# Opening loop of a graph layer: statistics one block at a time, loads spread between the stores, deeper table rows, list work in quarters

## The reference

```python
xn = _layernorm(x, axis=-1)                     # (6250, 256)
h  = (xn @ W).reshape(n, 8, 32)                 # L0_gnn
a1 = jnp.sum(h * attn_l, axis=-1); a2 = jnp.sum(h * attn_r, axis=-1)
e  = leaky_relu(a1[src] + a2[dst]);  out = segment_sum(h[src] * softmax_by_dst(e), dst)
q, k, v = split(xn_normalised @ Wqkv);  k = softmax(k, axis=nodes)      # L0_mix
```

## Time and profile before

| | |
|---|---|
| time, median of 3 runs | 6431.17 us (6430.95 to 6431.87) |
| time of the profiled execution | 6432.53 us, its span 6430.7 us |
| opening loop, first instruction of turn 0 to that of turn 48 (VectorE) | 19.93 to 185.11 us |
| mean granted clock of TensorE | 0.885 of full speed |
| busy in the whole span: TensorE, VectorE, GpSimd, ScalarE | 4977.0, 4128.9, 3649.1, 1548.3 us |

### The profile page before, as it was taken

The page is one execution under the profiler, slowest core; times in us unless marked ns, Lnnn a source line. Parts: engine busy times, 40 slices in busy tenths (PEclk is TensorE's granted clock), DMA queues, the critical chain, the costliest instruction groups (busy, mean ns, idle before and its releaser), DMA issues. The chain is left out here.

```text
span 6430.7 us, 105194 instructions
## 1 busy us (share of the span) xinstructions
PE 4977.0 (77%) x26438; PEld 3591.3 (56%) x26691; DVE 4128.9 (64%) x9565; ACT 1548.3 (24%) x3076; POOL 3649.1 (57%) x3844
## 2 busy tenths in 40 slices
PE   5867777777777776799799997777777777766694
PEld 4535555555555555798544444655555555555583
DVE  5438999998989898435650003877777777666444
ACT  1213333333333333454433331000000000000341
POOL 3447777777777773603200004777777777776524
PEclk8978999989888887799999998888888888888597
DMA  4424444444444443423344443333333333333345
GB/s 144 125 72 109 113 113 113 113 113 113 113 113 113 113 112 117 143 77 103 106 149 169 174 171 126 109 109 109 109 109 109 109 109 109 106 105 96 131 147 151
DMA packets 367220, 762.40 MB, mean 119 GB/s; under 512 B 92003, under 2 KB 232321, under 8 KB 354241
## 3 DMA queue, kind: packets, MB, share of 16 engines
q0 software_dynamic: 175104, 491.59, 27.1%
q1 hardware_dynamic: 184912, 262.86, 12.1%
q10 hardware_dynamic: 7056, 6.43, 0.3%
HBM read 562.75 MB, written 199.66 MB: 119 GB/s over the span
## 5 line engine op out<-in xcount | busy, mean ns | idle before, releaser
L868 POOL DMA_INDIRECT rg_ring<-y_dram,src_at x1612 | 1528.3, 948 | 1265.2 <-POOLq L906 774.3
L868 POOL DMA_INDIRECT ga_ring<-h_dram,src_at x1612 | 1532.6, 951 | 507.9 <-issue 460.8
L1716 PE MATMUL rg_psS<-rg_ring,rg_hot_w 128*128 x4000 | 1148.1, 451 | 397.7 <-SPq L844 304.2
L1716 PEld LDWEIGHTS rg_psS<-rg_ring,rg_hot_w 128*128 128x128 f32 x4000 | 902.0, 230 | 640.2 <-issue 478.1
L1042 PE MATMUL ga_psS<-ga_msg,ga_hot 128*128 128x280 f32 x4000 | 1194.1, 455 | 46.1 <-DVE ga_msg L1182 38.1
L1042 PEld LDWEIGHTS ga_psS<-ga_msg,ga_hot 128*128 128x128 f32 x4000 | 850.0, 221 | 313.9 <-DVE ga_msg L1182 88.6
L1833 DVE TENSOR_SCALAR rg_hot_t<-rg_psB,pair_node,place 128x1024 bf16<-128x1024 f32 x253 | 338.4, 1338 | 586.0 <-PE rg_psB L915 586.0
L1521 PE MATMUL rr_psY<-rr_wr,rr_xt 128*128 128x512 f32 x1568 | 675.1, 593 | 4.6 <-DMA rr_xt<-x_dram 4.6
L1182 DVE SCALAR_TENSOR_TENSOR ga_msg<-ga_psW,ga_ring 128x2112 f32<-128x2112 f32 x251 | 587.3, 2340 | 0.0
L1521 PEld LDWEIGHTS rr_psY<-rr_wr,rr_xt 128*128 128x128 f32 x1568 | 298.4, 190 | 379.0 <-issue 373.9
L2261 PE MATMUL f_psH<-f_xt,f_now 128*128 128x128 f32 x2688 | 351.3, 281 | 48.9 <-DVE f_now L2554 37.9
(11 more groups left out here) (403 smaller groups left out, 6694.3 us busy)
## 6 DMA issues: line engine op xcount, KB each, us to landing
y_dram<-rr_y SPq DMA_DIRECT2D x98, 1024.0 KB
f_x<-xg_dram SPq DMA_DIRECT2D x224, 128.0 KB
yg_dram<-f_work SPq DMA_DIRECT2D x224, 128.0 KB
ga_ring<-h_dram,src_at POOLq DMA_INDIRECT x1612
rg_ring<-y_dram,src_at POOLq DMA_INDIRECT x1612
rr_xt<-x_dram SPq DMA_DIRECT2D x98, 128.0 KB, 3.8
f_w<-L_ffn_W SPq DMA_DIRECT2D x16, 512.0 KB, 6.0
h_dram<-op_row SPq DMA_DIRECT2D x49, 136.0 KB, 1.8
```

The costliest lines, as they stand in the source:

```text
L868: p.indirect_dma_start(ring[:, (g % R) * G + j, :], None, table, bass.IndirectOffsetOnAxis(ap=rows[:, g * G + j:g * G + j + 1], axis=0)).t ...
L1716: o = pe.matmul(psS[:, u % 2, 0:C], hot_w[:, u % 2, j, :], rows[:, j, :], start=j == 0, stop=j == G - 1)
```

## The change

It changes only the opening's first block, apart from three counts in the next one.

- **Statistics.** The blocks are in seven groups of seven. `measure(b)` does one `bn_stats`; two follow each of turns 0 to 5, then one each turn, until turn 35. `spreads` (the small operations) follows turns 3, 7, 14, 21, 28 and 35, and `scales_of` (wait for the root, reciprocals) one turn later. ScalarE's `root_of` stands after turns 3, 7, 14, 21, 28 and 35.
- **Loads.** Two groups of x are loaded ahead of the loop, the others after the stores of turns 0, 2, 7, 12 and 17. The node list comes in four quarters after turns 9, 14, 18 and 20, the source list and late weights after turn 22. SyncE issues a turn's turned block ahead of its table row.
- **Table rows.** `row` has four buffers instead of two, with a semaphore each.
- **List work.** The node list's mask and conversion are done a quarter at a time, mask and conversion in alternate turns, over turns 24 to 31; the pair lists move to turn 23; the following lists are loaded after turn 32; the comparison is done in halves at turns 40 and 41, and the last lists are loaded after turn 44.
- The last weight tile `cbd` of the next block shares the memory of `wt`.

The core of the diff:

```diff
-    spans = [(0, 7), (7, 21), (21, NB)]
-    stats_at = {2: 1, 9: 2}
-    tables_at, rows_at, flags_at = 14, 24, 36
+    SPAN = 7
+    spans = [(lo, min(lo + SPAN, NB)) for lo in range(0, NB, SPAN)]
+    upto = [min(SPAN + 2 * (b + 1) if b < 6 else b + 14, NB) for b in range(NB)]
+    spread_at = {min(b for b in range(NB) if upto[b] >= hi): q for q, (_, hi) in enumerate(spans) if q}
+    loads_at = {0: 2, 2: 3, 7: 4, 12: 5, 17: 6}
+    held_at = (9, 14, 18, 20)
+    tables_at, rows_at, flags_at = 14, 24, 40
...
-        row = sb("row", [P, 2, HROW])
+        row = sb("row", [P, 4, HROW])
...
                 for b in range(NB):
-                    sp.wait_ge(rowed, b + 1)
-                    sp.dma_start(k.h_dram[b * P:(b + 1) * P, :], row[:, b % 2, :]).then_inc(stored[b % 2], 16)
                     sp.wait_ge(back, b + 1)
                     sp.dma_start(k.xt_dram[b * P:(b + 1) * P, :], xt[:, b % 4, :]).then_inc(turns_out[b % 4], 16)
+                    sp.wait_ge(rowed, b + 1)
+                    sp.dma_start(k.h_dram[b * P:(b + 1) * P, :], row[:, b % 4, :]).then_inc(stored[b % 4], 16)
+                    if b in loads_at:
+                        load(loads_at[b])
+                    if b in held_at:
+                        n = held_at.index(b)
+                        sp.dma_start(hold[:, n * GE:(n + 1) * GE], S["dst_twice"][n * P:(n + 1) * P, :]).then_inc(held, 16)
+                    if b == held_at[-1] + 2:
+                        sp.dma_start(k.src_at[:], S["src"]).then_inc(of_late, 16)
...
-                    if b == rows_at + 1:
+                    if b == rows_at + 2 * len(held_at):
                         sp.wait_ge(used, 1)
...
-                    if b == flags_at + 1:
+                    if b == flags_at + 4:
                         sp.wait_ge(used, 2)
...
-                    if b in stats_at:
-                        root_of(stats_at[b])
+                    if b in spread_at:
+                        root_of(spread_at[b])
...
+                def measure(b):
+                    if b % SPAN == 0:
+                        v.wait_ge(x_in[b // SPAN], 16)
+                    v.bn_stats(six[:, b, :], xv[:, b, 0:C])
+
+                def spreads(q):
                     lo, hi = spans[q]
...
-                    if b >= 2:
-                        v.wait_ge(stored[u], 16 * (b // 2))
+                    u, r = b % 2, b % 4
+                    if b >= 4:
+                        v.wait_ge(stored[r], 16 * (b // 4))
                     v.wait_ge(both, b + 1)
...
-                    if b in stats_at:
-                        stats(stats_at[b])
+                    if b - 1 in spread_at:
+                        scales_of(spread_at[b - 1])
+                    for m in range(upto[b - 1] if b else SPAN, upto[b]):
+                        measure(m)
+                    if b in spread_at:
+                        spreads(spread_at[b])
...
-                        v.tensor_tensor(hold[:], hold[:], parts[:].to_broadcast([P, z.CHUNKS * GE]), ALU.bitwise_and)
-                        v.drain()
-                        v.tensor_copy(k.node_rows[:], hold[:]).then_inc(used, 1)
+                    if rows_at <= b < rows_at + 2 * len(held_at):
+                        n, second = divmod(b - rows_at, 2)
+                        part = hold[:, n * GE:(n + 1) * GE]
+                        if second:
+                            t = v.tensor_copy(k.node_rows[:, n * GE:(n + 1) * GE], part)
...
+                        else:
+                            if n == 0:
+                                v.wait_ge(held, 16 * len(held_at))
+                            v.tensor_tensor(part, part, parts[:].to_broadcast([P, GE]), ALU.bitwise_and)
+                    if b == rows_at - 1:
                         v.wait_ge(tab3, 48)
...
-        cbd = sb("cbd", [P, KC, C])
+        cbd = wt
```

More of the change, by code:

```diff
@@ L216, in opening @@
             "staged", "turned", "back", "both", "kept", "rowed"))
-        stored = [sem("stored0"), sem("stored1")]
+        stored = [sem(f"stored{u}") for u in range(4)]
         turns_out = [sem(f"turns_out{u}") for u in range(4)]
@@ L269, in _ @@
                         sp.dma_start(others, S["dst_next"]).then_inc(held, 16)
-                for u in range(2):
-                    sp.wait_ge(stored[u], 16 * len(range(u, NB, 2)))
                 for u in range(4):
+                    sp.wait_ge(stored[u], 16 * len(range(u, NB, 4)))
                     sp.wait_ge(turns_out[u], 16 * len(range(u, NB, 4)))
@@ L379, in _ @@
                 v.tensor_copy(counti[:], counts[:]).then_inc(cvt, 1)
-                def stats(q):
+                def measure(b):
[3 more added lines that the diff above has]
+                def spreads(q):
                     lo, hi = spans[q]
-                    v.wait_ge(x_in[q], 16)
-                    for b in range(lo, hi):
-                        v.bn_stats(six[:, b, :], xv[:, b, 0:C])
                     v.drain()
@@ L401, in stats, with scales_of @@
                     o.then_inc(var_ready, 1)
+                def scales_of(q):
+                    lo, hi = spans[q]
                     v.wait_ge(root_ready, q + 1)
@@ L406, in stats @@
                     v.tensor_tensor(ratio[:, lo:hi], rstd[:, lo:hi], root[:, 1, lo:hi], ALU.mult).then_inc(scaled, 1)
-                stats(0)
+                for b in range(SPAN):
+                    measure(b)
+                spreads(0)
+                scales_of(0)
                 v.wait_ge(of_weights, 16 * 5)
@@ L472, in _ @@
                         v.tensor_scalar(k.pair_group[:], k.pair_group[:], z.NGT - 1, None, ALU.min)
-                    if b == flags_at:
-                        v.wait_ge(held, 48)
-                        v.tensor_tensor(starts[:], turns[:, 0, :], turns[:, 1, :], ALU.not_equal).then_inc(used, 1)
+                    if flags_at <= b < flags_at + 2:
+                        lo, hi = (z.ROWS * GE * (b - flags_at + q) // 2 for q in range(2))
+                        if b == flags_at:
+                            v.wait_ge(held, 16 * len(held_at) + 32)
+                        t = v.tensor_tensor(starts[:, lo:hi], turns[:, 0, lo:hi], turns[:, 1, lo:hi], ALU.not_equal)
+                        if b == flags_at + 1:
+                            t.then_inc(used, 1)
         ek = sb("ek", [P, 4, C])
@@ L581, in _ @@
                     if b == 8:
[L582 removed]
+                        v.wait_ge(held, 16 * len(held_at) + 64)
                         v.tensor_copy(k.dstf[:], ints)
```

34 lines of the change are left out of this document (16 added, 18 removed).

## The result

The changed kernel takes 6393.26 us (median; 6392.14 to 6394.91) where the kernel before takes 6431.06 beside it: a ratio of 0.9943, 95% interval 0.9931 to 0.9955, or 37.8 us less. 6396 was forecast, 35.4 less. The profiled execution spans 6391.6 us against 6430.7, 39.1 less. Turn 48 starts 35.3 us earlier; the other 3.8 lie behind the loop. That remainder took 6237.5 to 6245.9 us in the fourteen kernels of this study, which differ there at most in the lists loaded ahead of it and in which later tiles share memory; so 3.8 can't be told from its wander. So a question of a few us is settled by the length of the loop in one traced execution of each kernel, and the median tells only the whole.

What follows compares the result with a forecast made beforehand. No engine is always busy; chains ending in stores or VectorE's statistics stall the loop 69.2 us. Left over 6.7 + 1.4 + 13.2 + 12.0 + 0.5 = 33.8, a gain of 35.4: 6396 us, range 6379 to 6416.

Steps and rivals of the forecast that it cites:

- turns 0 to 5: Chain of statistics, spreads, root, reciprocals and GpSimd's block at turn 3: stall 4.7 plus 2.0 clock, 6.7 where 25.2 were.
- tables and turns 12 to 24: Spreads, table arithmetic, wait behind the table writes 7.4, clock 2.0, backlog: 13.2 us against 11.9 before.
- list work, 1 MB lists, to turn 48: Turns 23 to 32: VectorE 5.5 over, wait behind the 2 MB load 4.5, clock 2.0: 12.0 against 14.5.
- last lists, behind the loop: Last lists loaded at turn 44 instead of 37: the 3.68 idle goes, last stores end some 0.5 us later.
- so the deeper ring of table rows buys nothing here: Turns 12 to 24, at the table writes: ScalarE's ring is four deep in both kernels, so no gain from deeper table rows.
- The spread at turn 28 hides in that.: Turns 23 to 32: this spread adds nothing beyond VectorE's 5.5 us over, 23.5 of work for 18.0.
- The tables' price: Turns 12 to 24: 12.6 us from first table write to ScalarE's copy, as before; ScalarE waits 8.4, TensorE 7.4.
- The statistics: Turns 5 to 12: the third statistics block is gone, leaving a stall of 1.4 us of 13.3.
- Rival 1: Stores don't wait behind tables and lists, as one turn's earlier issue suffices: 9.4 and 6.5 go, 6380 us; chance 0.14.
- rival 2: SyncE's queue is the bound, loads between stores taking 27.9 us: 6410 with half on the path, 6424 with all; chance 0.12.
- rival 3: TensorE stays at the half clock, 1.98 us a turn; over turns 3 to 36 that gives 6456; chance 0.05.
- rival 4: Gain given back: the next loop waits at step 8 for lists loaded at turn 44, 6431 at worst; chance 0.06.

Runs made afterwards that it cites:

- u_row2: The changed kernel with table rows two deep again instead of four: 6405.81 us, ratio 0.9965, the loop 10.8 us longer.
- m_root: The changed kernel with ScalarE's root one turn later: 6388.35 us, ratio 0.9939, the loop 5.6 us shorter.
- m_ring8: The changed kernel with eight buffers instead of four for turned blocks and for table rows: 6384.9 us, ratio 0.9931, the loop 13.0 us shorter.
- m_tabq: The changed kernel with the six table writes issued by ScalarE through its own queue, after its output of turn 15: 6391.66 us, ratio 0.9941.
- u_stats: The changed kernel with three groups of statistics again, in bursts after turns 2 and 9, x in three loads: 6400.51 us, ratio 0.9957.
- u_loads: The changed kernel with all of x, the lists and late weights loaded ahead of the loop again: 6409.47 us, ratio 0.9972, the loop 14.0 us longer.
- t_one: The changed kernel with the six table writes made one transfer of the same 768 numbers: 6392.74 us, ratio 0.9944.

## Why the prediction was right, step by step

| term | forecast over | measured over | rows |
|---|---|---|---|
| turns 0 to 5 | 6.7 | 6.4 | idle 4.45 (4.7 said), slow turn +1.7 (2.0) |
| turns 5 to 12 | 1.4 | 1.7 | |
| tables and turns 12 to 24 | 13.2 | 15.0 | ScalarE's wait 8.74 (8.4), TensorE's 7.77 (7.4) |
| list work, 1 MB lists, to turn 48 | 12.0 | 11.1 | TensorE's wait 4.94 (4.5), slow turn +1.5 (2.0) |
| last lists, behind the loop | 0.5 | 1.5 | 5.1 from turn 48 to the next loop's product, 3.6 before |

The third and fourth line are to be taken together, 25.2 and 26.1, since the forecast put turn 23 with the list work. The sum was 33.8 against 35.8; the loop's own 34.3 is within 1 us of the 33.3 forecast for it. The first product behind the loop comes 33.8 us earlier (188.66 to 154.86), and the remainder of the 39.1 was not forecast and lies in the wander of the rest. So there is some luck in the total: at that product the gain was 33.8, short of the 35.4 forecast, and the rest of the program carried the time past it to 37.8. The terms were right within 2 us, because each was a chain of instructions with durations from rows, and because the clock's price was put behind each long stall. The loads that the forecast counted as just caught up left one wait of ScalarE for a landing, 1.29 at 93.30, of which TensorE felt 0.32. Four steps were not right:

- **"so the deeper ring of table rows buys nothing here"** held for the tables alone, and the prediction looked nowhere else. u_row2 shows 7.3 us of value in turns 31 to 48, of which 2.0 come back behind the loop. Behind the last lists ScalarE's ring of four just suffices, and VectorE's ring of two does not.
- **"The spread at turn 28 hides in that."** It does not: ScalarE waits 4.15 for it, TensorE 2.64, and the turn behind runs slow. VectorE works almost without a gap there, as said, but that makes it late: it begins turn 28 at 100.18, 1.8 behind ScalarE's output of that turn (98.36), and the spreads come after its own work of the turn. That the stretch is 5.6 over where 5.5 was said is luck, two errors that cancel: of the 5.5, the pair lists' 1.5 fall due in turn 23. m_root shows the mechanism. Even the slow turn is not certain there: in m_ring8 the same idle 2.64 leaves the granted clock at 1.00.
- **The tables' price** (12.6 us from issue to copy) was taken over from the kernel before and held (13.0), but the picture behind it, a store that waits its turn in SyncE's queue, fell with m_tabq: the store waits for the numbers to land, in whichever queue they go.
- **The statistics**: most of the gain that the prediction read at turns 5 to 12 is paid again later. u_stats shows 11.3 there and 10.4 back.

Rival 1 (tables cost nothing) is excluded by the 8.74, rival 2 by u_loads, rival 3 by the granted clock within the loop (of nine stretches from 20 to 150 us it is 0.89 to 1.00 in all but that from 72 to 80, 0.57), rival 4 by the 1.5 behind the loop. The rule of the Trainium skill (SBUF — State Buffer, section "SBUF: two separate sides") by which VectorE would lose up to a GpSimd block for each quarter is not borne out: the quarters took 1.33, 1.22, 1.22 and 1.25, and GpSimd worked beside all of them but the third, so it cost a quarter 0.11 at most. The rule of the Trainium skill of transfers of at least 1 MiB (DMA: Bandwidth & Descriptors, section "Bandwidth") would have spoken against the pieces of 896 KB. No run varies their size alone; their place between the stores is worth 14 us of the loop in u_loads, because of what stands behind them.

## What to carry to other kernels

Cost a loop by stretches, each as one chain from row to row, and add what the lower clock may take behind every long stall; then ask of each ring depth at every place where a transfer stands ahead, not at one. Work that is cut up and interleaved pays again at each point where an in-order engine waits for a piece of it, so move the waiting instruction a turn later along with the cut. A stall behind a transfer that resists being shortened, as the table writes did in m_tabq and t_one, may still be ridden out by a deeper ring: eight places instead of four took 13 us from this loop.

## What the runs showed of the hardware that was not expected

- 768 single numbers took 12.7 us from the first issue to the last landing (17.1 from ScalarE's queue), and a block stored behind them was back only then, from the same queue or another. In SyncE's queue it was back 11.6, 13.0 and 14.8 us after the first issue for one transfer, six, and twelve with twice the numbers; for 5 us of this 25 GB/s moved with the transfer engines busy at a share of 0.72.
- TensorE's granted clock fell from 1.00 to 0.50 in or right behind idle times of 2.64, 4.45, 4.94 and 7.77 us in the changed kernel, and did not behind 3.68 in the kernel before, 3.34 in m_tabq and the same 2.64 in m_ring8: the length of one idle time alone does not tell it.
- Issuing six small transfers took ScalarE's queue 3.40 us (2.83 on SyncE), in which ScalarE did nothing else.
